# The low halves of the conv input on VectorE instead of GpSimd

## What is computed

```python
perceived = conv_general_dilated(x, w_perc, padding='SAME', feature_group_count=128)   # 128 -> 384
hid = gelu(einsum('bphw,dp->bdhw', perceived, w_up1))                                  # 384 -> 256
x_new = x + einsum('bdhw,cd->bchw', hid, w_up2)                                        # 256 -> 128
q, k, v = split(einsum('bhwc,dc->bhwd', h_new, w_qkv), 3)
scores = stack([(q * shifted(k, dy, dx)).sum(-1) for dy, dx in the 9 places]) / sqrt(128)
w = softmax(scores)
out = h_new + sum_i w[i] * shifted(v, dy_i, dx_i)
```

## Time and profile before

| | us |
|---|---|
| median of three runs | 429.75 (428.68 to 431.12) |
| the profiled execution, device time | 428.88 |
| its span in the trace | 427.1 |
| PE busy in the span | 399.9 (94%) |
| VectorE busy | 342.2 (80%) |
| ScalarE busy | 271.3 (64%) |
| GpSimd busy | 169.9 (40%) |

### The profile page before, as it was taken

The page is one execution under the profiler, slowest core; times in us unless marked ns, Lnnn a source line. Parts: engine busy times, 40 slices in busy tenths (PEclk is TensorE's granted clock), DMA queues, the critical chain, the costliest instruction groups (busy, mean ns, idle before and its releaser), DMA issues.

```text
span 427.1 us, 9715 instructions
## 1 busy us (share of the span) xinstructions
PE 399.9 (94%) x3572; PEld 340.3 (80%) x3572; DVE 342.2 (80%) x656; ACT 271.3 (64%) x643; POOL 169.9 (40%) x155
## 2 busy tenths in 40 slices
PE   1397998999999999999999999999999999999895
PEld 1397695988879797888979798887979788896674
DVE  4997678796988969797897969798897969765666
ACT  5424358668475767747575865756576674856683
POOL 6577164242534434153534424353443425310100
PEclk9999999999999999999999999999999999999999
DMA  8210301031220404031130403122040401110003
GB/s 269 106 41 23 112 2 49 2 119 45 90 73 6 157 1 146 14 111 49 49 110 0 160 0 111 49 68 91 0 160 0 131 28 51 51 51 0 2 9 140
DMA packets 11366, 28.54 MB, mean 67 GB/s; under 512 B 2384, under 2 KB 3024, under 8 KB 11344
## 3 DMA queue, kind: packets, MB, share of 16 engines
q1 hardware_dynamic: 10640, 28.23, 19.4%
q10 hardware_dynamic: 704, 0.02, 0.1%
HBM read 19.85 MB, written 8.39 MB: 66 GB/s over the span
## 4 chain that ended last, share of the span: by engine, by line
PE 83%; DVE 4%; issue 2%; ACT 2%; POOL 0%; DVEq 0%; ACTq 0%
PE m_ps L416 42%; PE work L431 12%; PE work L471 8%; PE work L437 7%; PE work L442 6%; PE s_ps L455 6%; PE s_ps L451 2%; DVE y L823 1%; DVE y L826 1%; DVE ptc L877 1%; ACT hid L591 1%; DVE y L822 0%; DVE pt L892 0%; PE m_ps L471 0%; DVE y L828 0%
## 5 line engine op out<-in xcount | busy, mean ns | idle before, releaser
L416 PE MATMUL m_ps<-thi,whi 128*128 128x248 f32 (+1 forms) x576 | 178.7, 310 | 5.6 <-POOL wlo L1040 4.8
L416 PE MATMUL m_ps<-thi,wlo 128*128 128x248 f32 (+1 forms) x576 | 161.1, 280 | 0.0
L416 PE MATMUL m_ps<-tlo,whi 128*128 128x248 f32 (+1 forms) x576 | 160.3, 278 | 0.0
L416 PEld LDWEIGHTS m_ps<-thi,whi 128*128 128x128 f32 x576 | 109.2, 190 | 15.4 <-issue 12.0
L416 PEld LDWEIGHTS m_ps<-tlo,whi 128*128 128x128 f32 x576 | 109.7, 191 | 7.2 <-issue 7.2
L416 PEld LDWEIGHTS m_ps<-thi,wlo 128*128 128x128 f32 x576 | 108.9, 189 | 0.0
L1031 POOL TENSOR_TENSOR p_sb<-p_sb,rsum 128x384 f32<-128x384 f32 x32 | 27.8, 870 | 155.5 <-DVE rsum L866 155.5
L591 ACT ACTIVATE hid<-y,b1eff 128x1024 f32<-128x1024 f32 x31 | 35.7, 1151 | 79.3 <-DVE y L836 56.3
L1024 POOL TENSOR_TENSOR tlo<-t,thi 128x1024 fp32r<-128x1024 f32 (+1 forms) x32 | 60.3, 1906 | 54.1 <-ACT thi L575 54.1
L630 ACT COPY pt<-ptc 32x256 f32<-32x256 f32 (+3 forms) x189 | 74.1, 392 | 6.0 <-DVE ptc L877 1.4
L431 PE MATMUL work<-hid,w2T 128*128 128x512 f32 x120 | 54.1, 593 | 3.6 <-ACT hid L591 3.6
(11 more groups left out here) (109 smaller groups left out, 592.5 us busy)
## 6 DMA issues: line engine op xcount, KB each, us to landing
xp<-x_planes SPq DMA_DIRECT2D x16, 640.0 KB, 4.2
xr<-x_rows SPq DMA_DIRECT2D x16, 512.0 KB, 3.3
out<-o_sb SPq DMA_DIRECT2D x28, 256.0 KB, 2.0
out<-y SPq DMA_DIRECT2D x4, 256.0 KB, 2.1
w1T<-w SPq DMA_DIRECT2D x1, 384.0 KB, 3.1
w2T<-w SPq DMA_DIRECT2D x1, 128.0 KB, 4.3
wqk_in<-w_qk SPq DMA_DIRECT2D x1, 128.0 KB, 4.6
mask_bf<-masks SPq DMA_DIRECT2D x1, 120.0 KB, 3.5
```

Source lines behind the costliest of these rows:

```text
L416: last = pe.matmul(m_ps[:, b, col + first:col + end], a[:, j, dy, half * P:(half + 1) * P], c[:, par, T_PLACE[j], first + by:end + by], st ...
```

## The change

`low_t(n+1)` goes from GpSimd to VectorE for images 1 to 15. On VectorE it stands behind `transform(n+1)` and `sum_h(n)` and ahead of `combine_y(n, 0)`; both parts wait for ScalarE's `thi_done` as GpSimd's did. `low_t(0)` stays on GpSimd. Semaphores and their counts are unchanged.

```diff
+            def low_t(n, par):
+                for i, part in enumerate(T_PARTS):
+                    dve.wait_ge(thi_done, n * 2 + (i + 1))
+                    nc.vector.tensor_tensor(tlo[:, par, part, :], t[:, part, :], thi[:, par, part, :].bitcast(F32),
+                                            ALU.subtract).then_inc(tlo_done, 1)
...
                     transform(n + 1, 1 - par)
                 if from_image(n, 2) and attn:
                     sum_h(n, par)
+                if more:
+                    low_t(n + 1, 1 - par)
                 if conv:
                     combine_y(n, 0)
                     finish_y(n, 0)
...
                 if more:
                     differences(n + 1, 1 - par)
-                if more:
-                    for i in range(len(T_PARTS)):
-                        low_t(n + 1, 1 - par, i)
                 for c in range(NCH):
                     if attn:
                         normalise(n, c)
```

## The result

The changed kernel takes 435.97 us (median, 435.56 to 436.33) against 430.44 us (428.68 to 431.50) of the kernel before, measured beside it: a ratio of 1.0132, with a 95% interval of 1.0094 to 1.0171. It is slower, by 5.5 us between the medians. The forecast was slower, 434.0 us with a range to 436.0.

A forecast was written before the change was run, and what follows sets the result against it. The prediction took TensorE, busy 94% of the span, to bound the kernel. Startup delays of 2.2 us in body 0 and 2.1 in body 1, steady images at nothing, gave 429.75 + 4.3 = 434.0 us, range 431.4 to 436.0.

The forecast's parts named there:

- What bounds the kernel: Whole kernel: TensorE, busy for 94% of the span; steady-image changes count only if they make it wait anew.
- Price of the moved work: Both parts of low_t on VectorE, from start to start: 1.73 us per image.
- Body 0: First image: low_t(1) waits for thi(1), finish_y(0, 0) starts 4.2 us later, leaving 2.2 us at up(1).
- the turns with `differences(2)`: Body 0: GpSimd's differences(2) starts earlier, beside low_t(1), and the engines alternate; finish_y(0, 0) 4.2 us later, without turns 3.0.
- Body 1: Second image: VectorE idles 3.9 us for thi(2), ScalarE's GELU and take_m13(1, 1) come late; 2.1 us at up(2).
- the sum of 4.3 us: Startup terms of bodies 0 and 1, 2.2 + 2.1 us; steady images, tail and start before body 0 at nothing.
- My upper bound: If low_t cost VectorE GpSimd's 3.6 us, both startup terms grow by 1.9: 8.1 in all, 437.9 us.
- Faster by relief: Steady images: VectorE's 1.4 us relief comes back in 13 images, 18 less 4.3, 416 us; chance 0.06.
- Only one term arrives: Bodies 0 and 1: just one startup term of 1.0 to 2.1 us shows, about 431.3 us; chance 0.13.
- No turns in body 0: Body 0: VectorE and GpSimd do not alternate, its term is 1.0 us, total 432.9 us; chance 0.14.
- A late `thi` in every image: Steady images: VectorE waits for thi before combine_y, 4 us more over 13 images, 438 us; chance 0.05.

The follow-up runs named there:

- e4: Changed kernel with low_t(1) and low_t(2) back on GpSimd, images 3 to 15 on VectorE; 429.27 us, ratio 0.9979 to the kernel before.
- e5: Changed kernel with GpSimd's differences(2) held back until y_done(0, 0); 434.16 us.
- e1: Changed kernel with 34 extra matmuls that nothing reads, filling most of TensorE's wait ahead of unit 10 of image 0; 433.16 us.
- e2: Changed kernel with low_t(1), in body 0, back on GpSimd, all other images on VectorE; median 435.0 us, profiled execution 432.84.
- e3: Changed kernel with low_t(2), in body 1, back on GpSimd, all other images on VectorE; 432.87 us.
- e8: Kernel before with 16 extra matmuls ahead of up(1) and 13 ahead of up(2), filling TensorE's two waits; median 429.23 us, ratio 0.9978.
- e6: Changed kernel with low_t(n+1) later in VectorE's queue, behind row_max(n, 0), in body 0 behind finish_y(0, 0); 429.55 us, ratio 0.9979.
- e7: The kernel of e2 run once more, nothing else changed; 433.46 us.

## Why the prediction was right and where it was wrong

**What bounds the kernel.** Right. In the kernel before TensorE is busy for 24.00 of 24.00 us with its clock at 1.00 in each of the twelve stretches from 84 to 372 us. Full rows of TensorE meant that the steady part is worth nothing in either direction; e4 has the same floor as the kernel before, and from `up(2)` to the end the traces are 361.3 us long in all three.

**Price of the moved work.** Right: 1.73 us forecast, 1.74 measured, from a 768-wide and a 256-wide row.

**Body 0.** The wait for `thi(1)`, the turns with `differences(2)` that had come loose, and the delay of `finish_y(0, 0)`: 4.2 forecast, 4.22 measured, and e5 gives the turns' share as 1.3 of it (1.2 was forecast). The delay that is left at `up(1)` at full clock: 2.2 forecast, 2.11 in e1.

**Body 1.** 2.1 forecast, 2.13 in e2, by ScalarE's chain as described: its GELU waits for `finish_y(1, 0)`, and four `exp` and the table load push `take_m13(1, 1)` (61.10 and 64.86 in the rows above). The wait of TensorE ahead of the last `project_v`, 1.6 forecast, is 1.40.

**Wrong: the sum of 4.3 us.** The step "TensorE then has work up to `up(1)`, where it has 1.98 us of waiting to give: 4.2 - 2.0 = 2.2" priced that work at the duration it has in the profile before. But the wait of 4.5 us ahead of unit 10 had its own consequence: TensorE's granted clock fell to 0.50, and the matmuls of units 10 and 11 and most of the first unit of the next image started 0.21 us apart instead of 0.12, until 44.2 us. In the profiled executions it cost 2.4 us in the changed kernel and 1.6 in e3, and it is nothing in e1. So the shift at `up(2)` was 6.5 and not 4.3. Between the medians it is 5.5, because the kernel before also loses about 2 us in many of its executions, which e8 and the profile of e4 put down to such a fall (two of the four measured beside the changed kernel and 31 of 54 beside the experiments are in its slower group). Its single profile, with the clock at 1.00 and full spacing through bodies 0 to 2 once TensorE had come up, did not show it. The profiled executions are 7.45 us apart: 6.51 at `up(2)` and the 0.95 ahead of the first combine.

Two waits of 0.3 and 2 us turned into one of 4.5, and the sum has no term for the clock in bodies 0 to 2; the clock of 1.00 in the earlier trace rows is that of a steady stretch. My upper bound was for the price of `low_t`, which two rows of VectorE had already given. The unknown one was how fast TensorE's matmuls would be behind a wait of 4.5 us.

**The rivals.** Faster by relief: refuted by e4. Only one term arrives: refuted by the traces of e2 and e3, each of which keeps its own (2.13, and 2.0 beside 1.6 of clock). No turns in body 0: refuted by e5. A late `thi` in every image: the only waits of VectorE for `thi` in the changed kernel are the two of bodies 0 and 1, 4.9 us together.

**What stays open.** In e2 six of seven executions took 434.7 to 435.8 us and none of these was profiled; two falls of the clock, at `up(1)` and `up(2)`, would explain them, and their lower mean clock goes with it, but no trace shows both in one execution. The two executions of e1 at 435.5 were not profiled either. Which executions fall after a wait of 2 us cannot be told from these runs.

## What to carry to other kernels

Work that is moved to another engine brings its waits along, and they count for everything that is queued behind them; the same two instructions cost 5.5 us between the medians ahead of `combine_y` and nothing a few instructions later (e6, 429.55 us). Look for this at the first iterations, where a hand-written order differs from the steady loop and the margins that the steady trace shows are missing. Behind waits of TensorE of 1.98 to 4.50 us its clock read 0.50 in some of these profiles and 1.00 in others; where a change brings such a wait, price the matmuls behind it both ways (here 0.21 and 0.12 us from start to start). When a queue gets shorter, ask what moves up in it and whom that meets: `differences(2)` beside `low_t(1)` cost 1.3 us here (e5).

## What the runs showed of the hardware

- TensorE's granted clock fell to 0.50 in or right after waits of 4.50 us (changed kernel, e3), 2.48 (e6), 2.06 to 2.08 (e2, e5, e7) and 1.98 (e4), and stayed at 1.00 after waits of 3.21 us (e5), 2.07 and 2.06 (the changed kernel and e1 at `up(2)`) and 1.98 (before, and e2 at `up(1)`). One fall cost 1.4 (e6) to 2.4 us (the changed kernel). The 34 matmuls of no use that kept TensorE at work through most of the wait of 4.50 us in e1 were a gain: 2.8 us between the medians.
- `low_t` and `combine_y` on VectorE took turns with `fc` and `ge` on GpSimd: 1.83 us (e5, apart) became 2.53 (the changed kernel, beside each other) for the two subtractions, 0.42 became 0.97 for the first `combine_y` instruction, and 0.69 and 0.76 became 1.65 and 1.20 for GpSimd's two `ge`. ScalarE's GELU and VectorE's `finish_y`, which reads an accumulator bank, took the same: in body 0 of the kernel before 1.16 and 0.68 us beside GpSimd's `low_t(1)`, and in the changed kernel, with GpSimd idle, 1.15 and 0.67.
